# A graph network with attention on one core: argument in node order, a new step order, one subtraction on VectorE

## The chip, the cores and the metric

One core of a Trainium2 chip runs the whole kernel in one launch. The metric is the device time of that launch in microseconds (us). TensorE is called PE in the profile, VectorE DVE, ScalarE ACT, GpSimd POOL, and SyncE, whose queue issues the DMAs, SP; PEld is TensorE's weight load.

## The reference, cut to what matters

The input x is (16, 512, 256): 16 batches of 512 nodes with 256 features, and one 0/1 adjacency of 512 x 512 for all of them.

```
h   = relu(layernorm(x))
for 4 heads:  Wh = h @ W[head];  e[i,j] = leaky(f1[i] + f2[j]), masked by adj
              out[head] = softmax(e) @ Wh                       # f1 = Wh.a1, f2 = Wh.a2
h   = elu(concat of the heads)                                  # 512 x 1024
out = elu(the same attention once more, one head, W_out)        # the "back" head
y   = relu(out @ w1 + b1) @ w2 + b2 + out
x   = x + layernorm(y) * gamma + beta
h   = relu(layernorm(x))
x   = x + deg * (h @ Wi + b) + adj @ (h @ Wj)                   # graph convolution
```

Everything is fp32. The large products are made of three fast products each, hi x hi + lo x hi + hi x lo, where hi is the value rounded by ScalarE's copy (type fp32r) and lo is what is left, value - hi.

## The kernel before, in words

A batch passes through some forty steps on TensorE. Its attention is cut into ten units: four heads with two halves of 256 rows each, and the back head with two halves. UNITS (L233) numbers them: 0 to 3 are heads 0 and 1, 4 and 5 the back head of the batch before, 6 to 9 heads 2 and 3.

Each engine has a table of steps written out by hand at the top of the file: (name, info, late). The tables are walked once per wave, and a step works in wave t on batch t - late. So several batches are in flight, each engine runs its table strictly in order, and semaphores hold a step until its operands are there. The order in which work meets is set by these five tables alone.

A unit's way: `rowmax` on VectorE (L619) adds the broadcast f2 row (tile f2bc) to the mask, writes arg, and takes the row's maximum; `rowmath` (L629) makes two small vectors of it; `args` on ScalarE (L435) applies the leaky slope and the exponential; `rinv` and `scale` on VectorE (L645, L649) normalize; `turn_p` on TensorE (L774) transposes arg into PSUM in eight pieces; `probs` on ScalarE (L447) and on VectorE (L638) split it into prob_hi and prob_lo; `attend` on TensorE (L784) multiplies, 24 matmuls; `elu_neg` and `elu_exp` on ScalarE (L456, L467) and `elu_out` on VectorE (L656) form elu. For the four front heads `hx` on ScalarE (L471) rounds it to hx_hi, and `hx_lo` on GpSimd (L376) subtracts to get hx_lo. `mix2` on TensorE (L801) multiplies these by W_out, 24 matmuls for each 128 rows; it waits for hx_lo of the last head, for the first half before its steps 0 and 1, for the second before 2 and 3.

There are three arg buffers, two f2bc rows, two prob buffers and two elu buffers. `elu_neg` waits until the hx_lo of the unit two before has been made. PSUM is four pairs of banks: each TensorE step takes the pair that was taken longest ago, and waits until its last user has been read out (take and lend, L732 to L739).

The columns of arg are not in node order. x is loaded with node c * 128 + p in chunk c, partition p, and the f2 row is written to DRAM as (q c), so that its four chunks are interleaved. The mask is made in the same interleaved order, `rowmax` works on plain rows, and `turn_p` takes every fourth column of arg for each transposed piece. The norms' powers, `add_b2`, `gamma` and `x_beta` also run on GpSimd (L370 to L396). VectorE has two kinds of elementwise work that matter here: instructions with one operand in PSUM (`probs`, `elu_out`, `m1`) and instructions with both in SBUF (`rowmax`, `x2`).

The other steps: `m1` (L762) makes Wh and f1, f2 of a head for two chunks of rows, 12 matmuls; `f2send` and `f2bcast` on SP (L317, L331) write the f2 column to DRAM and read it back on all partitions; `ffn1`, `ffn2` (L825, L834), `turn_in`, `turn_out`, `turn_gc` (transposes), `conv_in` (L854) and `conv` (L865) are the rest; `store` and `load_back` on SP (L343, L338) write xb and fill it with the next batch's x.

## Time and profile before

| | |
|---|---|
| time, median of 3 | 1514.7 us (1514.22 to 1515.41) |
| the profiled execution's own time | 1505.55 us |
| its span | 1503.5 us |
| PE busy | 1339.4 us (89%), 9944 matmuls |
| PE weight loads | 1260.0 us (84%) |
| DVE busy | 1190.4 us (79%) |
| ACT busy | 1083.5 us (72%) |
| POOL busy | 349.2 us (23%) |
| chain that ended last | PE 51%, DVE 35%, issue 6%, ACT 5%, POOL 2% |

Busy time is the union of an engine's instructions. A matmul's duration in the profile is longer than the distance to the next, since they are pipelined: the distance (0.12 us for 256 columns) is what one costs. The span runs from the first to the last recorded work; the own time adds what lies around it.

### The profile page before, as it was taken

How to read it: one execution, taken by the hardware profiler on the slowest of the kernel's cores; microseconds unless marked ns; L12 is line 12 of the kernel's file. 1: busy time of each engine (PE TensorE's matmuls, PEld its weight loads, DVE VectorE, ACT ScalarE, POOL GpSimd, SP SyncE). 2: the span in 40 equal slices, each digit the busy share in tenths (PEclk: the TensorE clock that was granted, in tenths of full speed). 3: DMA queues.
4: the chain of work that ended last, by engine and by line, in shares of the span. 5: the costliest groups of instructions: out<-in, count | busy, mean ns of one | idle time of the engine just before them, and what ended most of it. 6: DMA issues, size and time to landing. Idle time of an engine off the chain costs nothing.

```text
span 1503.5 us, 27090 instructions
## 1 busy us (share of the span) xinstructions
PE 1339.4 (89%) x9944; PEld 1260.0 (84%) x9944; DVE 1190.4 (79%) x2833; ACT 1083.5 (72%) x2037; POOL 349.2 (23%) x234
## 2 busy tenths in 40 slices
...
DMA packets 53091, 54.07 MB, mean 36 GB/s; under 512 B 14048, under 2 KB 41696, under 8 KB 52832
## 3 DMA queue, kind: packets, MB, share of 16 engines
...
## 4 chain that ended last, share of the span: by engine, by line
PE 51%; DVE 35%; issue 6%; ACT 5%; POOL 2%; DMA 2%; POOLq 0%; ACTq 0%; DVEq 0%; SPq 0%
PE ps L747 33%; DVE arg L625 12%; PE ps L780 5%; DVE prob_lo L606 4%; DVE arg L653 4%; PE ps L830 4%; PE ps L871 4%; PE ps L840 3%; DVE elu L661 2%; DVE zneg L633 2%; DVE whx_lo L606 2%; DVE st L587 1%; POOL hx_lo L378 1%; DVE xb L699 1%; PE ps L849 1%
## 5 line engine op out<-in xcount | busy, mean ns | idle before, releaser
L378 POOL TENSOR_TENSOR hx_lo<-elu,hx_hi 128x512 fp32r<-128x512 f32 x128 | 171.2, 1338 | 622.7 <-ACT hx_hi L474 622.7
L747 PE MATMUL ps<-prob_hi,whx_hi 128*128 128x256 f32 x1024 | 298.5, 291 | 11.4 <-DVE wk L661 7.6
L747 PE MATMUL ps<-prob_lo,whx_hi 128*128 128x256 f32 x1024 | 289.7, 283 | 0.0
L747 PE MATMUL ps<-prob_hi,whx_lo 128*128 128x256 f32 x1024 | 289.2, 282 | 0.0
L625 DVE CUSTOM_DVE_ANT_0 arg<-f2bc,mask 128x512 f32<-128x512 f32 x320 | 278.7, 907 | 1.9 <-DMA f2bc<-f_rows 1.6
L444 ACT ACTIVATE arg<-arg,nmax 128x512 f32<-128x512 f32 x320 | 227.7, 718 | 0.6 <-DVE nmax L636 0.5
L440 ACT ACTIVATE arg<-arg,fcol 128x512 f32<-128x512 f32 x320 | 213.5, 721 | 12.1 <-DVE gmax L625 12.1
L780 PE MATMUL ps<-ident,arg 128*128 128x128 f32 x1280 | 186.9, 290 | 36.9 <-DVE arg L653 32.4
L747 PEld LDWEIGHTS ps<-prob_hi,whx_hi 128*128 128x128 f32 x1024 | 196.1, 192 | 17.2 <-issue 9.7
L780 PEld LDWEIGHTS ps<-ident,arg 128*128 128x128 f32 x1280 | 170.6, 209 | 45.0 <-DVE arg L653 34.8
L450 ACT ACTIVATE prob_hi<-ps 128x1024 fp32r<-128x1024 f32 x160 | 163.4, 1021 | 58.7 <-PE ps L747 33.1
L606 DVE TENSOR_TENSOR prob_lo<-ps,prob_hi 128x1024 fp32r<-128x1024 f32 x160 | 194.7, 1217 | 12.5 <-ACT prob_hi L450 9.8
L747 PEld LDWEIGHTS ps<-prob_hi,whx_lo 128*128 128x128 f32 x1024 | 195.6, 191 | 0.4
L747 PEld LDWEIGHTS ps<-prob_lo,whx_hi 128*128 128x128 f32 x1024 | 195.5, 191 | 0.0
L747 PE MATMUL ps<-wo_hi,hx_hi 128*128 128x258 f32 x512 | 146.0, 285 | 22.9 <-POOL hx_lo L378 22.9
L653 DVE TENSOR_SCALAR arg<-arg,rinv 128x512 f32<-128x512 f32 x320 | 153.5, 521 | 1.9
L747 PE MATMUL ps<-wh_hi,hT_hi 128*128 128x258 f32 x512 | 150.9, 295 | 2.4 <-DVE hT_lo L606 2.4
L747 PE MATMUL ps<-wh_lo,hT_hi 128*128 128x258 f32 x512 | 145.8, 285 | 0.0
L747 PE MATMUL ps<-wh_hi,hT_lo 128*128 128x258 f32 x512 | 145.4, 284 | 0.0
L747 PE MATMUL ps<-wo_lo,hx_hi 128*128 128x258 f32 x512 | 144.4, 282 | 0.0
L747 PE MATMUL ps<-wo_hi,hx_lo 128*128 128x258 f32 x512 | 143.8, 281 | 0.0
L433 ACT ACTIVATE whx_hi<-ps 128x512 fp32r<-128x512 f32 x128 | 75.8, 592 | 88.5 <-PE ps L747 88.5
...
## 6 DMA issues: line engine op xcount, KB each, us to landing
...
f_rows<-fcol SPq DMA_DIRECT2D x80, 2.0 KB, 3.4
...
```

Of the source, the lines that this page charges most:

```text
L378: pool.tensor_tensor(out=hx[1][:, 2 * c.h:2 * c.h + 2, c.u * HN:(c.u + 1) * HN], in0=elu[:, c.buf, :, :], in1=hx[0][:, 2 * c.h:2 * c.h + 2 ...
L433: act.activation(whx[:, 2 * p:2 * p + 2, h, 0:F], pairs[c.pair][:, :, 0:F], ACT.Copy).then_inc(m1_hi, 1)
L440: act.activation(a[:, n, :], a[:, n, :], ACT.Prelu, bias=f1[:, n:n + 1], alpha=SLOPE).then_inc(arg_lin, 1)
L444: i = act.activation(a[:, n, :], a[:, n, :], ACT.Exp, bias=nmax[:, c.abuf, n:n + 1], accum_out=rsum[:, c.abuf, n:n + 1])
L450: act.activation(prob[0][:, c.buf, :, :].rearrange("p j i -> p (j i)"), pairs[c.pair][:, :, :].rearrange("p a n -> p (a n)"), ACT.Copy).th ...
L606: return dve.tensor_tensor(out=dst, in0=src, in1=hi.bitcast(fp32), op=ALU.subtract)
L625: dve.tensor_tensor_reduce(out=arg[:, c.abuf, n, :], in0=f2bc[:, head % F2S, :], in1=mask[:, 2 * c.u + n, :], scale=1.0, scalar=-3.0e38, o ...
L653: i = dve.tensor_scalar(arg[:, c.abuf, n, :], arg[:, c.abuf, n, :], rinv[:, c.abuf, n:n + 1], None, ALU.mult)
L747: i = pe.matmul(out, a, b_, start=(k == 0), stop=(k == n - 1))
L780: i = pe.transpose(p[:, j, n, :], arg[:, c.abuf, n, :].rearrange("p (q c) -> p c q", c=NC)[:, j, :], ident[:, :])
L830: i = pe.matmul(pairs[c.pair][:, o, :], w1_sb[:, k, o * P:(o + 1) * P], outT[:, k, :], start=(k == 0), stop=(k == KC - 1))
L871: i = pe.matmul(pairs[c.pair][:, n // 2, (n % 2) * F:(n % 2 + 1) * F], adjT[:, j, n * P:(n + 1) * P], mj, start=(j == 0 and s == 0), stop= ...
```

## The change

Three edits. The argument is in node order now: `rowmax` reads f2bc through a view that takes every fourth element, and writes plain rows; the mask is built in node order by one instruction; `turn_p` transposes plain slices. `hx_lo` is computed by VectorE, as a step in its table, and no more by GpSimd. All five tables have a new order, with some steps one or two waves later (`turn_in` 1 where it was 0, `conv` 6 where it was 4). ScalarE's table, left out below, has the same steps as before in a new order.

```diff
--- before.py
+++ after.py
@@ -5,52 +5,51 @@
 
 
 SP_STEPS = [
-    ("f2send", -1, 3), ("load", 0, 0), ("f2send", 2, 2), ("f2bcast", -1, 3), ("f2send", 3, 2), ("f2bcast", 2, 2),
-    ("store", 0, 5), ("f2bcast", 3, 2), ("f2send", 0, 1), ("load_back", 0, 4), ("f2send", 1, 1), ("f2bcast", 0, 1),
+    ("f2send", -1, 3), ("f2bcast", -1, 3), ("f2send", 2, 2), ("f2send", 3, 2), ("f2bcast", 2, 2), ("f2send", 0, 1),
+    ("load", 0, 0), ("f2bcast", 3, 2), ("store", 0, 5), ("load_back", 0, 4), ("f2send", 1, 1), ("f2bcast", 0, 1),
     ("f2bcast", 1, 1),
 ]
 PE_STEPS = [
-    ("m1", (1, 1), 1), ("attend", 5, 3), ("turn_p", 7, 2), ("attend", 6, 2), ("turn_p", 8, 2), ("m1", (2, 0), 1),
-    ("attend", 7, 2), ("m1", (2, 1), 1), ("turn_p", 9, 2), ("attend", 8, 2), ("turn_out", 0, 3), ("m1", (3, 0), 1),
-    ("attend", 9, 2), ("mix2", 0, 2), ("mix2", 1, 2), ("mix2", 2, 2), ("mix2", 3, 2), ("m1", (3, 1), 1), ("turn_p", 0, 1),
-    ("turn_in", 0, 0), ("ffn1", 0, 3), ("turn_gc", 0, 4), ("turn_p", 1, 1), ("attend", 0, 1), ("conv_in", 0, 4),
-    ("conv_in", 1, 4), ("turn_p", 2, 1), ("m1", (0, 0), 0), ("attend", 1, 1), ("turn_p", 3, 1), ("ffn2", 0, 3),
-    ("attend", 2, 1), ("m1", (0, 1), 0), ("conv", 0, 4), ("turn_p", 4, 2), ("attend", 3, 1), ("turn_p", 5, 2),
-    ("m1", (1, 0), 0), ("turn_p", 6, 1), ("attend", 4, 2),
+    ("conv", 0, 6), ("turn_p", 5, 4), ("m1", (1, 1), 2), ("turn_p", 6, 3), ("attend", 4, 4), ("turn_p", 7, 3),
+    ("attend", 5, 4), ("attend", 6, 3), ("turn_p", 8, 3), ("attend", 7, 3), ("turn_p", 9, 3), ("turn_out", 0, 4),
+    ("attend", 8, 3), ("m1", (2, 0), 2), ("m1", (2, 1), 2), ("attend", 9, 3), ("ffn1", 0, 4), ("mix2", 0, 3),
+    ("turn_gc", 0, 5), ("turn_p", 0, 2), ("mix2", 1, 3), ("mix2", 2, 3), ("mix2", 3, 3), ("ffn2", 0, 4), ("m1", (3, 0), 2),
+    ("m1", (3, 1), 2), ("turn_p", 1, 2), ("turn_in", 0, 1), ("conv_in", 0, 5), ("attend", 0, 2), ("turn_p", 2, 2),
+    ("turn_p", 3, 2), ("attend", 1, 2), ("m1", (0, 0), 1), ("m1", (0, 1), 1), ("conv_in", 1, 5), ("attend", 2, 2),
+    ("turn_p", 4, 3), ("m1", (1, 0), 1), ("attend", 3, 2),
 ]
 ACT_STEPS = [
...
 DVE_STEPS = [
-    ("m1", (1, 1), 3), ("elu_out", 5, 5), ("probs", 7, 4), ("rinv", 9, 4), ("scale", 9, 4), ("elu_out", 6, 4),
-    ("probs", 8, 4), ("m1", (2, 0), 3), ("elu_out", 7, 4), ("m1", (2, 1), 3), ("rowmax", 0, 3), ("probs", 9, 4),
-    ("elu_out", 8, 4), ("rowmath", 0, 3), ("norm_gc", 0, 6), ("rowmax", 1, 3), ("rowmath", 1, 3), ("rowmax", 2, 3),
-    ("elu_out", 9, 4), ("rowmath", 2, 3), ("m1", (3, 0), 3), ("mix2", 0, 4), ("rinv", 0, 3), ("scale", 0, 3), ("rinv", 1, 3),
-    ("norm_gc_out", 0, 6), ("scale", 1, 3), ("mix2", 1, 4), ("m1", (3, 1), 3), ("probs", 0, 3), ("rowmax", 3, 3),
-    ("turn_in", 0, 2), ("rinv", 2, 3), ("rowmath", 3, 3), ("turn_gc", 0, 6), ("scale", 2, 3), ("probs", 1, 3),
-    ("norm_in", 0, 1), ("conv_in", 0, 6), ("rinv", 3, 3), ("elu_out", 0, 3), ("scale", 3, 3), ("conv_in", 1, 6),
-    ("probs", 2, 3), ("rowmax", 4, 4), ("rowmath", 4, 4), ("m1", (0, 0), 2), ("rowmax", 5, 4), ("rowmath", 5, 4),
-    ("probs", 3, 3), ("elu_out", 1, 3), ("rowmax", 6, 3), ("ffn2", 0, 5), ("rinv", 4, 4), ("rowmath", 6, 3),
-    ("norm_ff", 0, 5), ("scale", 4, 4), ("rinv", 5, 4), ("elu_out", 2, 3), ("m1", (0, 1), 2), ("conv", 0, 6),
-    ("norm_ff_out", 0, 5), ("scale", 5, 4), ("rowmax", 7, 3), ("rinv", 6, 3), ("norm_in_out", 0, 1), ("scale", 6, 3),
-    ("probs", 4, 4), ("rowmath", 7, 3), ("elu_out", 3, 3), ("probs", 5, 4), ("rowmax", 8, 3), ("m1", (1, 0), 2),
-    ("rinv", 7, 3), ("rowmath", 8, 3), ("scale", 7, 3), ("probs", 6, 3), ("x2", 0, 5), ("elu_out", 4, 4), ("rowmax", 9, 3),
-    ("rowmath", 9, 3), ("rinv", 8, 3), ("scale", 8, 3),
+    ("x2", 0, 6), ("elu_out", 4, 5), ("probs", 7, 4), ("rinv", 9, 4), ("scale", 9, 4), ("elu_out", 5, 5), ("elu_out", 6, 4),
+    ("probs", 8, 4), ("rowmax", 0, 3), ("hx_lo", 6, 4), ("elu_out", 7, 4), ("probs", 9, 4), ("rowmath", 0, 3),
+    ("rowmax", 1, 3), ("hx_lo", 7, 4), ("norm_gc", 0, 6), ("elu_out", 8, 4), ("rowmax", 2, 3), ("norm_gc_out", 0, 6),
+    ("rinv", 0, 3), ("hx_lo", 8, 4), ("rowmath", 1, 3), ("m1", (2, 0), 3), ("scale", 0, 3), ("m1", (2, 1), 3),
+    ("elu_out", 9, 4), ("rowmath", 2, 3), ("rowmax", 3, 3), ("hx_lo", 9, 4), ("rowmath", 3, 3), ("turn_gc", 0, 6),
+    ("norm_in", 0, 2), ("rinv", 1, 3), ("mix2", 0, 4), ("scale", 1, 3), ("rinv", 2, 3), ("rinv", 3, 3),
+    ("norm_in_out", 0, 2), ("scale", 2, 3), ("mix2", 1, 4), ("scale", 3, 3), ("probs", 0, 3), ("ffn2", 0, 5),
+    ("norm_ff", 0, 5), ("m1", (3, 0), 3), ("m1", (3, 1), 3), ("probs", 1, 3), ("turn_in", 0, 2), ("conv_in", 0, 6),
+    ("rowmax", 4, 4), ("rowmath", 4, 4), ("rowmax", 5, 4), ("elu_out", 0, 3), ("probs", 2, 3), ("rowmax", 6, 3),
+    ("probs", 3, 3), ("rowmath", 5, 4), ("rinv", 4, 4), ("elu_out", 1, 3), ("scale", 4, 4), ("hx_lo", 0, 3),
+    ("m1", (0, 0), 2), ("conv_in", 1, 6), ("m1", (0, 1), 2), ("rowmath", 6, 3), ("rowmax", 7, 3), ("rinv", 5, 4),
+    ("norm_ff_out", 0, 5), ("elu_out", 2, 3), ("hx_lo", 1, 3), ("rowmath", 7, 3), ("rinv", 6, 3), ("scale", 5, 4),
+    ("probs", 4, 4), ("scale", 6, 3), ("m1", (1, 0), 2), ("conv", 0, 6), ("elu_out", 3, 3), ("rowmax", 8, 3), ("rinv", 7, 3),
+    ("rowmath", 8, 3), ("probs", 5, 4), ("scale", 7, 3), ("m1", (1, 1), 2), ("hx_lo", 2, 3), ("rowmax", 9, 3),
+    ("probs", 6, 3), ("rowmath", 9, 3), ("rinv", 8, 3), ("hx_lo", 3, 3), ("scale", 8, 3),
 ]
 POOL_STEPS = [
-    ("hx_lo", 7, 4), ("hx_lo", 8, 4), ("norm_gc", 0, 6), ("add_b2", 0, 5), ("hx_lo", 9, 4), ("norm_in", 0, 1),
-    ("hx_lo", 0, 3), ("hx_lo", 1, 3), ("norm_ff", 0, 5), ("gamma", 0, 5), ("hx_lo", 2, 3), ("x_beta", 0, 5), ("hx_lo", 3, 3),
-    ("hx_lo", 6, 3),
+    ("norm_ff", 0, 6), ("gamma", 0, 6), ("x_beta", 0, 6), ("norm_gc", 0, 6), ("norm_in", 0, 2), ("add_b2", 0, 5),
 ]
 
 
@@ -373,11 +372,6 @@
                     pool.tensor_tensor(out=rstd[k][:, :], in0=mv[k][:, :, 1], in1=mhalf[:, :], op=ALU.pow).then_inc(ln_rstd[k], 1)
                 return step
 
-            def hx_lo_(c):
-                pool.wait_ge(hx_hi, head_unit(c.b, c.h, c.u) + 1)
-                pool.tensor_tensor(out=hx[1][:, 2 * c.h:2 * c.h + 2, c.u * HN:(c.u + 1) * HN], in0=elu[:, c.buf, :, :],
-                                   in1=hx[0][:, 2 * c.h:2 * c.h + 2, c.u * HN:(c.u + 1) * HN].bitcast(fp32), op=ALU.subtract).then_inc(hx_lo, 1)
-
             def add_b2(c):
                 if c.b == 0:
                     pool.wait_ge(ld[LD_B2], 16)
@@ -398,7 +392,7 @@
             for l in (LD_G, LD_BE):
                 pool.wait_ge(ld[l], 16)
             pool.wait_ge(s_setup, 1)
-            run_all(POOL_STEPS, {"norm_in": norm("in"), "hx_lo": hx_lo_, "add_b2": add_b2, "x_beta": x_beta_,
+            run_all(POOL_STEPS, {"norm_in": norm("in"), "add_b2": add_b2, "x_beta": x_beta_,
                                  "norm_ff": norm("ff"), "gamma": gamma_, "norm_gc": norm("gc")})
 
         @block.scalar
@@ -516,10 +510,7 @@
 
             dve.wait_ge(ld[LD_ADJ], 16)
             link(dve.tensor_copy(adj_f, adj_f.bitcast(i32)))
-            for n in range(NC):
-                i = dve.tensor_scalar(mask[:, n, :].rearrange("p (q c) -> p c q", c=NC), adj_f[:, n, :].rearrange("p (c q) -> p c q", c=NC),
-                                      0.0, 1.0, ALU.is_gt, ALU.mult)
-            i.then_inc(s_adj, 1)
+            dve.tensor_scalar(mask[:, :, :], adj_f, 0.0, 1.0, ALU.is_gt, ALU.mult).then_inc(s_adj, 1)
             dve.wait_ge(s_adj, 1)
             link(dve.tensor_reduce(out=cnt, in_=mask[:, :, :], axis=AX.X, op=ALU.add))
             link(dve.tensor_scalar(lone, cnt, 0.0, 2.0 * BIG, ALU.is_equal, ALU.mult))
@@ -622,7 +613,9 @@
                 dve.wait_ge(f2_spread[head % F2S], 16 * (head // F2S + 1))
                 wait(dve, p_turned, c.unit - ARGS + 1)
                 for n in range(2):
-                    dve.tensor_tensor_reduce(out=arg[:, c.abuf, n, :], in0=f2bc[:, head % F2S, :], in1=mask[:, 2 * c.u + n, :],
+                    dve.tensor_tensor_reduce(out=arg[:, c.abuf, n, :].rearrange("p (c q) -> p c q", c=NC),
+                                             in0=f2bc[:, head % F2S, :].rearrange("p (q c) -> p c q", c=NC),
+                                             in1=mask[:, 2 * c.u + n, :].rearrange("p (c q) -> p c q", c=NC),
                                              scale=1.0, scalar=-3.0e38, op0=ALU.add, op1=ALU.max,
                                              accum_out=gmax[:, c.abuf, n:n + 1]).then_inc(max_made, 1)
 
@@ -666,6 +659,11 @@
                 ps, n = pairs[c.pair], 2 * c.info
                 lo(w2l[:, n:n + 2, :], ps[:, :, 0:F], w2x[:, n:n + 2, 0:F]).then_inc(m2_lo, 1)
                 dve.tensor_copy(fcol2[:, :, n:n + 2].rearrange("p s n -> p n s"), ps[:, :, F:FA]).then_inc(m2_read, 1)
+
+            def hx_lo_(c):
+                dve.wait_ge(hx_hi, head_unit(c.b, c.h, c.u) + 1)
+                dve.tensor_tensor(out=hx[1][:, 2 * c.h:2 * c.h + 2, c.u * HN:(c.u + 1) * HN], in0=elu[:, c.buf, :, :],
+                                   in1=hx[0][:, 2 * c.h:2 * c.h + 2, c.u * HN:(c.u + 1) * HN].bitcast(fp32), op=ALU.subtract).then_inc(hx_lo, 1)
 
             def ffn2(c):
                 dve.wait_ge(f2_done, c.b + 1)
@@ -701,7 +699,7 @@
 
             run_all(DVE_STEPS, {"norm_in": norm("in", xin, x_loaded, 16), "norm_in_out": norm_out("in"), "turn_in": turn_in, "m1": m1,
                                 "rowmax": rowmax, "rowmath": rowmath, "rinv": rinv_, "scale": scale, "probs": probs,
-                                "elu_out": elu_out_, "mix2": mix2, "ffn2": ffn2,
+                                "elu_out": elu_out_, "hx_lo": hx_lo_, "mix2": mix2, "ffn2": ffn2,
                                 "norm_ff": norm("ff", wk, y_ready, 1), "norm_ff_out": norm_out("ff"), "x2": x2,
                                 "norm_gc": norm("gc", xb, x2_ready, 1), "norm_gc_out": norm_out("gc"),
                                 "turn_gc": turn_gc, "conv_in": conv_in_, "conv": conv})
@@ -777,7 +775,7 @@
                 p = pairs[c.pair][:, :, :].rearrange("p a n -> p (a n)").rearrange("p (j n i) -> p j n i", j=NC, n=2)
                 for j in range(NC):
                     for n in range(2):
-                        i = pe.transpose(p[:, j, n, :], arg[:, c.abuf, n, :].rearrange("p (q c) -> p c q", c=NC)[:, j, :], ident[:, :])
+                        i = pe.transpose(p[:, j, n, :], arg[:, c.abuf, n, j * P:(j + 1) * P], ident[:, :])
                 i.then_inc(p_turned, 1)
                 lend((c.pair,), (prob_lo, c.unit + 1))
 
```

## Rows read from the trace of the kernel before

**Rows 1.** Windows, steady stretch: PE, PEld, DVE, ACT, POOL busy us; clock; DMA; GB/s
```profile
150.00:1350.00 1200.00, 1133.98 (x8556) 1071.47 (x8555) 1002.24 (x2355) 933.81 (x1768) 296.52 (x190) 1.00 0.13 33
```

**Rows 2.** Timeline of GpSimd, one line twelve batches apart: start us, us
```profile
270.00 2.43 POOL L385 TENSOR_TENSOR wk<-wk,b_bc 128x1024 f32<-128x1024 f32 x1
...
1312.87 2.43 POOL L385 TENSOR_TENSOR wk<-wk,b_bc 128x1024 f32<-128x1024 f32 x1
```

**Rows 3.** Chain of waits, 700 to 800 us: start us, us, engine, what, count
```profile
702.26 0.60 DVE arg L625
...
716.79 0.98 PE ps L780 x8
717.77 0.87 PE ps L758 x8
718.64 3.44 PE ps L830 x8
...
728.65 1.40 PE ps L747 x6
...
732.84 0.95 PE ps L780 x8
733.79 4.32 PE ps L747 x36
...
739.07 3.46 PE ps L840 x16
...
746.84 3.85 PE ps L871 x32
```

**Rows 4.** Who waited for whom, whole run: us in total, times, longest us
```profile
POOL hx_lo L378 <- ACT hx_hi L474: 622.7, 113, 26.1
...
PE ps L747 <- POOL hx_lo L378: 22.9, 14, 2.0
...
PE ps L747 <- DVE elu L661: 18.2, 14, 1.4
```

**Rows 5.** Instructions of single lines: ns min/median/max, first and last start us, form
```profile
L780 PEld LDWEIGHTS ps<-ident,arg x1280: 195/209/231, 62.3 to 1427.9; 128*128 128x128 f32 x183
...
L758 PEld LDWEIGHTS ps<-ident,xin x128: 139/143/231, 37.6 to 1241.1; 128*128 128x128 f32 x128
...
L625 DVE CUSTOM_DVE_ANT_0 arg<-f2bc,mask x320: 674/685/2899, 55.7 to 1419.3; 128x512 f32<-128x512 f32 x160
...
L679 DVE TENSOR_TENSOR xb<-xb,wk x16: 1207/1208/2280, 246.3 to 1473.6; 128x1024 f32<-128x1024 f32 x16
...
L378 POOL TENSOR_TENSOR hx_lo<-elu,hx_hi x128: 1262/1292/1678, 85.2 to 1393.5; 128x512 fp32r<-128x512 f32 x128
```

**Rows 6.** Timeline of VectorE in the setup: start us, us
```profile
6.14 1.23 DVE L518 CAST arg<-arg 128x2048 f32<-128x2048 int32 x1 [6.14 <-DMA arg<-in_adj]
7.40 2.45 DVE L520 TENSOR_SCALAR mask<-arg 128x512 bf16<-128x512 f32 x4
```

**Rows 7.** Timelines of VectorE and GpSimd, two places where they meet
```profile
703.23 2.87 DVE L625 CUSTOM_DVE_ANT_0 arg<-f2bc,mask 128x512 f32<-128x512 f32 x1
...
703.11 2.44 POOL L385 TENSOR_TENSOR wk<-wk,b_bc 128x1024 f32<-128x1024 f32 x1
...
783.18 1.77 DVE L625 CUSTOM_DVE_ANT_0 arg<-f2bc,mask 128x512 f32<-128x512 f32 x1
...
782.73 1.67 POOL L378 TENSOR_TENSOR hx_lo<-elu,hx_hi 128x512 fp32r<-128x512 f32 x1 [1.11 <-ACT hx_hi L474]
```

**Rows 8.** Groups by line, VectorE: count, busy us, mean ns, idle before us
```profile
L625 DVE CUSTOM_DVE_ANT_0 arg<-f2bc,mask 128x512 f32<-128x512 f32 x320 | 278.7, 907 | 1.9 <-DMA f2bc<-f_rows 1.6
```

**Rows 9.** Chain of waits, the end of the run
```profile
1464.35 2.91 DMA out_x<-xb
...
1493.44 0.61 ACT h2T_hi L500
...
1494.81 4.11 PE ps L871 x32
```

More of the change, by code:

```diff
@@ L20 @@
+    ("turn_gc", 0, 5), ("turn_p", 0, 2), ("mix2", 1, 3), ("mix2", 2, 3), ("mix2", 3, 3), ("ffn2", 0, 4), ("m1", (3, 0), 2),
+    ("m1", (3, 1), 2), ("turn_p", 1, 2), ("turn_in", 0, 1), ("conv_in", 0, 5), ("attend", 0, 2), ("turn_p", 2, 2),
+    ("turn_p", 3, 2), ("attend", 1, 2), ("m1", (0, 0), 1), ("m1", (0, 1), 1), ("conv_in", 1, 5), ("attend", 2, 2),
+    ("turn_p", 4, 3), ("m1", (1, 0), 1), ("attend", 3, 2),
 ]
 ACT_STEPS = [
-    ("probs", 4, 3), ("norm_ff_out", 0, 4), ("elu_neg", 3, 2), ("hx", 2, 2), ("elu_exp", 3, 2), ("probs", 5, 3),
@@ L23 @@
-    ("m1", (1, 0), 1), ("args", 7, 2), ("probs", 6, 2), ("elu_neg", 4, 3), ("hx", 3, 2), ("elu_exp", 4, 3), ("args", 8, 2),
-    ("elu_neg", 5, 3), ("m1", (1, 1), 1), ("probs", 7, 2), ("elu_exp", 5, 3), ("args", 9, 2), ("elu_neg", 6, 2),
-    ("elu_exp", 6, 2), ("probs", 8, 2), ("m1", (2, 0), 1), ("elu_neg", 7, 2), ("hx", 6, 2), ("m1", (2, 1), 1),
-    ("elu_exp", 7, 2), ("hx", 7, 2), ("probs", 9, 2), ("elu_neg", 8, 2), ("elu_exp", 8, 2), ("turn_out", 0, 3), ("hx", 8, 2),
-    ("elu_neg", 9, 2), ("m1", (3, 0), 1), ("elu_exp", 9, 2), ("hx", 9, 2), ("norm_in_out", 0, 0), ("args", 0, 1),
@@ L28 @@
-    ("mix2", 0, 2), ("args", 1, 1), ("mix2", 1, 2), ("norm_gc_out", 0, 4), ("m1", (3, 1), 1), ("probs", 0, 1),
-    ("turn_in", 0, 0), ("args", 2, 1), ("turn_gc", 0, 4), ("ffn1", 0, 3), ("probs", 1, 1), ("args", 3, 1), ("elu_neg", 0, 1),
-    ("elu_exp", 0, 1), ("conv_in", 0, 4), ("conv_in", 1, 4), ("probs", 2, 1), ("hx", 0, 1), ("m1", (0, 0), 0),
-    ("elu_neg", 1, 1), ("probs", 3, 1), ("elu_exp", 1, 1), ("args", 4, 2), ("args", 5, 2), ("elu_neg", 2, 1), ("hx", 1, 1),
-    ("elu_exp", 2, 1), ("m1", (0, 1), 0), ("args", 6, 1),
+    ("args", 4, 4), ("probs", 3, 3), ("elu_neg", 1, 3), ("m1", (0, 0), 2), ("hx", 0, 3), ("elu_exp", 1, 3),
@@ new lines @@
+    ("conv_in", 1, 6), ("m1", (0, 1), 2), ("args", 5, 4), ("elu_neg", 2, 3), ("hx", 1, 3), ("elu_exp", 2, 3), ("args", 6, 3),
+    ("probs", 4, 4), ("elu_neg", 3, 3), ("m1", (1, 0), 2), ("elu_exp", 3, 3), ("args", 7, 3), ("probs", 5, 4), ("hx", 2, 3),
+    ("hx", 3, 3), ("m1", (1, 1), 2), ("norm_ff_out", 0, 5), ("probs", 6, 3), ("args", 8, 3), ("elu_neg", 4, 4),
+    ("probs", 7, 3), ("elu_exp", 4, 4), ("elu_neg", 5, 4), ("args", 9, 3), ("elu_neg", 6, 3), ("elu_exp", 5, 4),
+    ("elu_exp", 6, 3), ("probs", 8, 3), ("hx", 6, 3), ("elu_neg", 7, 3), ("elu_exp", 7, 3), ("probs", 9, 3),
```

5 lines of the change are left out of this document (added).

## The prediction

> **What bounds the kernel now.** I read the windows first, then the chain of waits inside one batch, then the table of who waited for whom, then the groups by line, and last the two engines that touch each other, instruction by instruction.
>
> Away from the ends TensorE is busy 94% of the time at full clock, VectorE 84%, ScalarE 78%, GpSimd 25% [rows 1]. The batches repeat: the same GpSimd instruction starts at 270.00 and, twelve batches on, at 1312.87 [rows 2], so one batch takes 1042.87 / 12 = 86.9 us.
>
> How much of this is TensorE work? From the chain: `attend` issues 24 matmuls, 36 take 4.32 us, so 2.88 us; ten of them 28.8. Eight `m1` are 96 such matmuls, 11.5; four `mix2` another 96, 11.5. Ten `turn_p` at 0.96 are 9.6. `ffn1` 3.44, `ffn2` 3.46, `conv` 3.85, `conv_in` 4 x (1.40 + 0.12 for its bias) = 6.1, three other turns at 0.87, 2.6 [rows 3]. Sum 80.9. So 86.9 - 80.9 = 6.0 us per batch is idle, and the engine is the bound, but not at its floor. VectorE is busy 1002.24 us in 1200, 72.6 us per batch [rows 1]: 14 us of room.
>
> What ends TensorE's idle time: over the run 22.9 us for `hx_lo` from GpSimd (14 times, about 1.6 us each), 18.2 us for `elu_out` (14 times) [rows 4].
>
> **The change part by part.**
>
> *Transposes of plain slices.* The weight loads of `turn_p` read every fourth element now: 209 ns median, against 143 ns for the loads of plain slices of `xin` [rows 5]. Loads overlap matmuls, so this difference isn't the price. The chain has it: eight transposes of arg take 0.95 to 0.98 us, eight of `xin` 0.87 [rows 3]. That is 0.09 us x 160 = 14 us of the bounding engine. Ends: 0 (the loads hide wholly, and the step in the chain is some other start-up) and 160 x 0.11 = 18. I take 14, the middle of the two rows.
>
> *rowmax reads f2bc at every fourth element.* 320 instructions, now 685 ns median, 0.60 us apart in the chain [rows 3, 5]. The trace has no VectorE instruction of size with an input strided so. Ends: 0, and twice the time, a bound from the difference between 0.60 and 1.20 us. I take 0, since the instruction isn't quick enough to press on its reads: it passes 2048 elements in 4 x 0.60 = 2.4 us, where the plain conversion of 2048 took 1.23. And the nearest strided VectorE row, the writing of mask with gaps, takes 2.45 us for four, 0.61 apart, like the unstrided rowmax [rows 6]. The high end is a rival below.
> The Trainium skill speaks against this choice: SBUF — State Buffer, section "Door 1: The DMA port swizzle", says that an SBUF line has 16 bytes and that at least two hits on a line are needed for full bandwidth, while it also calls a stride of four fp32 free. By the first sentence the edit costs VectorE time, by the second nothing. The trace shows only TensorE's loads slower (209 against 143), and that does not decide it.
>
> *mask in natural order.* Four instructions, 2.45 us, become one over the same 2048 elements [rows 6]. The plain conversion beside it took 1.23 us, so up to 1.2 are saved, at the start, where all waits for VectorE. I take 1; ends 0 and 1.2.
>
> *hx_lo leaves GpSimd.* 128 instructions of 1292 ns median go [rows 5]. On VectorE one costs 0.60 us: 512 elements with two fp32 inputs; x2, the same form with 1024, takes 1208 ns [rows 5]. 128 x 0.60 = 77 us added, 4.8 per batch. It also takes a load off VectorE: a two-input instruction from SBUF stands still while GpSimd works. Rowmax takes 2.87 us when it starts 0.12 after a 2.44 us addition on GpSimd, and 1.77 us beside an `hx_lo` [rows 7]. By line, rowmax loses (907 - 685) ns x 320 = 71 us to this [rows 5, 8]. `hx_lo` makes up 128 x 1.29 = 165 us of GpSimd's large instructions, the additions 48 x 2.44 = 117, so its part by time is 58%, 41 us. So net VectorE gets 77 - 41 = 36 us, 2.2 per batch: 72.6 becomes 74.8. The rest of the lock stays, with three GpSimd operations of this kind per batch (`add_b2`, `gamma`, `x_beta`), and `hx_lo` can now be hit by it itself; ends of the net load 77 - 71 = 6 and 77 + 117, every addition's time lost in full.
> The skill's SBUF — State Buffer, section "Who interferes with whom", gives the rule: a VectorE instruction with two SBUF inputs and a GpSimd one that reads SBUF exclude each other for the whole instruction. The trace agrees (2.87 us against a median of 685 ns), and by it the moved subtraction becomes one more victim of the additions that stay.
>
> *The wait for hx_lo.* The last batch half needed is unit 9, and `mix2` 2 needs it. Before, two `mix2` stand between `attend` 9 and `mix2` 2: 5.7 us, and the operand comes 1.6 us late. In the new order `ffn1`, two `mix2`, `turn_gc` and one `turn_p` stand there: 3.44 + 5.74 + 0.87 + 0.96 = 11.0 us. The path (two ScalarE passes, elu_out, hx, hx_lo) took 5.7 + 1.6 = 7.3 and gets 0.7 shorter, as 0.60 replaces 1.27. VectorE has only `rowmath` 2, `rowmax` 3 (1.5 us) ahead of `hx_lo` 9. So 22.9 us go, and 2 us of room are left. Ends 0 and 23.
>
> *The order otherwise.* Between `turn_p` and `attend` of a unit TensorE has other work that must cover ScalarE's 1.02 and VectorE's 1.22 us. Summed over the tables with the durations above: unit 0 before, `turn_in`, `ffn1`, `turn_gc`, `turn_p`, 6.1 us; after, three `mix2`, `ffn2`, two `m1`, `turn_p`, `turn_in`, `conv_in`, 19.8. Mean of the ten units 7.7 before, 9.5 after; the smallest 5.1 and 4.6. A PSUM pair is taken again after at least 3.3 us of other work in both. So the average handoff is looser, the tightest no better, while VectorE is fuller. I book -3 us, ends -55 (period 82.5, 2.5 idle) and +30.
>
> *SP.* `load_back` now follows `store` directly, and waits for its 2.9 us [rows 9] with `f2send` 1 and `f2bcast` 0 and 1 behind it. Before, `f2bcast` 3 and `f2send` 0 stood between. `rowmax` 0, which needs the broadcast, comes in the next wave, some 20 us later; nothing is booked, and if that cover failed it would be up to 3 us a batch.
>
> *The ends.* `turn_in` of a batch to its `conv` is 4.3 waves in both tables, so the fill stays. In the drain `ffn2` of the last batch moves ahead of the conv of the one before. Before, it covers the wait of `conv` for the last lo part; the very last batch shows this wait bare, from 1493.44 to 1494.81, 1.4 us [rows 9]. The chain from that conv over store, reload, the addition and the last conv is unchanged. Booked +1.
>
> Sum: -14 - 23 - 1 - 3 + 1 = -40 us, that is about 2.6 us less per batch. The profiled execution took 1505.55 us, 1503.5 of it span, and would take 1465.5. The median of the runs is 1514.7, 9 us above it; with the same difference 1474.7, say 1475.
>
> **The rivals.**
>
> A, *VectorE becomes the bound through the strided read*. For it: TensorE's strided load is 209 / 143 = 1.46 times as long [rows 5]. At 1.46, 0.28 us x 320 = 88 us, 5.5 per batch: VectorE 80.3, TensorE 80.0, and with the 6 us of idling that the leader has today 86.3: 1514.7 - 0.6 x 15 = 1506. At twice the time 192 us, 12.0 per batch, 86.8 + 6 = 92.8: 5.9 x 15 = +88, 1603. It decides from about 0.3 us per instruction. Against it: at 0.60 us the instruction takes longer than its reads need, by the conversion's row. The two-hits rule of the Trainium skill (SBUF — State Buffer, section "Door 1: The DMA port swizzle") would be its cause.
>
> B, *VectorE, in order, waits for ScalarE's hx*. GpSimd could sit out 622.7 us for `hx_hi` [rows 4]; VectorE can't. Place: between `elu_out` u and `hx_lo` u the new table has 1.5 us (units 8, 9) to 10 us of other work, and ScalarE must get through hx in its own queue. If each of 128 waits cost 0.7 us, that is 5.6 per batch, VectorE 80.4, and as TensorE's waits for it grow with each late release, the period 86.4 + 1.1 (half of the 2.2 added in work) = 87.5: 0.6 x 15 = +9, 1524. Below about 0.3 us each it disappears in the room.
>
> C, *the idle time only moves*: the 6 us come back elsewhere, only the transposes stay: 1514.7 - 14 = 1501, or with a worse drain 1513.
>
> D, *the looser order pays in full*: period 82.5, 1514.7 - 4.4 x 15 - 9 = 1440.
>
> **How the numbers follow.** Forecast 0.50 (1455 to 1500), A 0.20, B 0.12, C 0.06, D 0.12. A difference is told from none at 0.2%, 3 us. Faster: 0.50 + 0.12 + 0.03 of A (a small penalty) + 0.03 of C = 0.68; same 0.02 + 0.02 + 0.03 = 0.07; slower 0.15 + 0.10 = 0.25. Range 1435 to 1540: below, all of D but its tail; above, all of B and the lower part of A. The forecast's own range is 1455 to 1500.
>
> **What would show it.** Right: rowmax's median still near 685 ns; `turn_p` loads near 143 ns; no TensorE wait for hx_lo above a few us in total; VectorE near 75 us per batch; one batch about 84.3 us by the starts of the GpSimd addition. Wrong: a rowmax median of 0.9 us or more (A); a VectorE row "hx_lo waits for hx_hi" of over 80 us (B); the transposes' step unchanged, or a batch still at 86 us with no engine fuller (C).

## The result, and the profile after

The changed kernel takes 1554.93 us (median of 4, 1554.57 to 1555.77) beside 1514.46 us for the kernel before: ratio 1.0268, interval 1.0252 to 1.0284. It is slower; 1475 us was forecast, and the range ended at 1540. The profiled execution has a span of 1553.1 us.

The windows of the steady stretch in the changed kernel, as in [rows 1]: time of PE, PEld, DVE, ACT, POOL, then clock.

```profile
150.00:1350.00 1200.00, 1115.05 (x8383) 1047.92 (x8382) 1101.56 (x2414) 922.54 (x1728) 139.31 (x77) 0.99 0.12 33
```

VectorE is busy 92% of the time now, TensorE 93% with fewer matmuls in the same 1200 us (8383 for 8556). The batches, by the same GpSimd addition as in [rows 2], ten batches apart in the changed kernel:

```profile
297.19 2.70 POOL L379 TENSOR_TENSOR wk<-wk,b_bc 128x1024 f32<-128x1024 f32 x1
...
1189.64 2.70 POOL L379 TENSOR_TENSOR wk<-wk,b_bc 128x1024 f32<-128x1024 f32 x1
```

(1189.64 - 297.19) / 10 = 89.2 us per batch, for 86.9. VectorE's part of it is 1101.56 / 1200 x 89.2 = 81.9 us. The single lines, answering to [rows 5], ns min/median/max:

```profile
L616 DVE CUSTOM_DVE_ANT_0 arg<-f2bc,mask x320: 1051/1096/3195, 54.6 to 1460.5; 128x512 f32<-128x512 f32 x160
...
L778 PEld LDWEIGHTS ps<-ident,arg x1280: 137/141/231, 62.8 to 1470.8; 128*128 128x128 f32 x183
```

Rowmax went from 685 to 1096 ns; the loads of the transposes from 209 to 141. In the chain of waits between 700 and 800 us a rowmax instruction takes 1.01 to 1.03 us, for 0.60 in [rows 3]; eight transposes take 0.87 in the second of the two rows, for 0.95 to 0.98:

```profile
706.22 1.03 DVE arg L616
707.26 1.01 DVE arg L616
...
713.21 1.07 PE ps L778 x8
...
717.45 0.87 PE ps L778 x8
```

Who waited, answering to [rows 4]: no row of TensorE's matmuls waiting for hx_lo is left (its weight loads keep 4.2 us). Its largest wait is now that of `turn_p` for `scale`, the last VectorE step of a unit before it. The second row goes the other way: rowmax waits until a transpose has freed an arg buffer. So neither engine bounds the kernel alone; of the chain that ended last TensorE has 47% and VectorE 45%, for 51% and 35% before.

```profile
PE ps L778 <- DVE arg L646: 54.5, 21, 11.2
...
DVE arg L616 <- PE ps L778: 52.3, 30, 2.8
...
PE ps L745 <- DVE prob_lo L597: 41.4, 29, 2.7
```

And VectorE's setup, as in [rows 6]:

```profile
7.54 1.23 DVE L513 TENSOR_SCALAR mask<-arg 128x2048 bf16<-128x2048 f32 x1
```

The mask costs 1.23 us for 2.45, as booked (1 us). VectorE's `hx_lo` (L665) is 845 ns in the mean and waited only 1.7 us in all for hx_hi:

```profile
L665 DVE TENSOR_TENSOR hx_lo<-elu,hx_hi 128x512 fp32r<-128x512 f32 x128 | 108.2, 845 | 1.7 <-ACT hx_hi L468 1.7
```

### The profile page after: what moved, and what is told of

Read it like the earlier page. It is cut to its first block, busy times and chain, and to the rows that moved or that the text cites. A ratio compares the mean times of both kernels' runs of the same rounds, so it can differ in the third digit from the quotient of the medians.

```text
span 1553.1 us, 27087 instructions
## 1 busy us (share of the span) xinstructions
PE 1353.6 (87%) x9944; PEld 1265.6 (81%) x9944; DVE 1330.9 (86%) x2958; ACT 1092.4 (70%) x2037; POOL 172.8 (11%) x106
## 4 chain that ended last, share of the span: by engine, by line
PE 47%; DVE 45%; issue 4%; ACT 2%; DMA 2%; POOL 0%; DVEq 0%; POOLq 0%; SPq 0%; ACTq 0%
PE ps L745 32%; DVE arg L616 13%; DVE prob_lo L597 6%; DVE arg L646 5%; PE ps L778 4%; PE ps L869 4%; PE ps L828 4%; DVE hx_lo L665 3%; DVE st L578 2%; DVE shift_in L592 2%; DVE elu L654 1%; DVE whx_lo L597 1%; DVE h2T_lo L597 1%; PE ps L847 1%; DVE w2x_lo L597 1%
## 5 line engine op out<-in xcount | busy, mean ns | idle before, releaser
L616 DVE CUSTOM_DVE_ANT_0 arg<-f2bc,mask 128x512 f32<-128x512 f32 x320 | 346.7, 1123 | 56.8 <-PE ps L778 52.3
L745 PE MATMUL ps<-prob_hi,whx_hi 128*128 128x256 f32 x1024 | 298.9, 292 | 37.2 <-DVE prob_lo L597 27.2
L745 PE MATMUL ps<-prob_hi,whx_lo 128*128 128x256 f32 x1024 | 293.3, 286 | 0.0
L778 PE MATMUL ps<-ident,arg 128*128 128x128 f32 x1280 | 170.4, 280 | 60.8 <-DVE arg L646 54.5
L778 PEld LDWEIGHTS ps<-ident,arg 128*128 128x128 f32 x1280 | 146.4, 144 | 67.9 <-DVE arg L646 59.3
L745 PEld LDWEIGHTS ps<-prob_hi,whx_lo 128*128 128x128 f32 x1024 | 199.7, 195 | 1.2
L745 PEld LDWEIGHTS ps<-prob_lo,whx_hi 128*128 128x128 f32 x1024 | 199.6, 195 | 0.0
L459 ACT ACTIVATE elu<-ps 128x512 f32<-128x512 f32 x160 | 94.9, 593 | 103.7 <-PE ps L745 71.7
L646 DVE TENSOR_SCALAR arg<-arg,rinv 128x512 f32<-128x512 f32 x320 | 166.8, 563 | 0.7
L745 PEld LDWEIGHTS ps<-wo_hi,hx_hi 128*128 128x128 f32 x512 | 96.6, 189 | 19.2 <-issue 15.0
```

The costliest lines, as they stand in the source:

```text
L459: act.activation(elu[:, c.buf, :, :], pairs[c.pair][:, :, 0:F], ACT.Relu, scale=-1.0).then_inc(elu_neg, 1)
L616: dve.tensor_tensor_reduce(out=arg[:, c.abuf, n, :].rearrange("p (c q) -> p c q", c=NC), in0=f2bc[:, head % F2S, :].rearrange("p (q c) -> ...
L646: i = dve.tensor_scalar(arg[:, c.abuf, n, :], arg[:, c.abuf, n, :], rinv[:, c.abuf, n:n + 1], None, ALU.mult)
L745: i = pe.matmul(out, a, b_, start=(k == 0), stop=(k == n - 1))
L778: i = pe.transpose(p[:, j, n, :], arg[:, c.abuf, n, j * P:(j + 1) * P], ident[:, :])
```

## The experiments

Theory 1: the read of f2bc at 16-byte steps lengthens rowmax, and VectorE's added time is the loss. Theory 2: hx_lo in VectorE's queue, or the new order, costs the time. The runs below were made on several chips. The kernel before, run beside each, took 1510.7 to 1514.9 us in the median, so differences between two runs are uncertain by up to some 4 us; each ratio is against the kernel before on the same chip.

**The argument edit, alone and left out.** `b_arg_only` is the kernel before with the strided rowmax, the mask in one instruction, and plain transposes. `c_no_arg` is the changed kernel with these three undone:

```diff
-                    dve.tensor_tensor_reduce(out=arg[...].rearrange("p (c q) -> p c q", c=NC), in0=f2bc[...].rearrange("p (q c) -> p c q", c=NC), ...
+                    dve.tensor_tensor_reduce(out=arg[:, c.abuf, n, :], in0=f2bc[:, head % F2S, :], in1=mask[:, 2 * c.u + n, :],
-   pe.transpose(p[:, j, n, :], arg[:, c.abuf, n, j * P:(j + 1) * P], ident[:, :])
+   pe.transpose(p[:, j, n, :], arg[:, c.abuf, n, :].rearrange("p (q c) -> p c q", c=NC)[:, j, :], ident[:, :])
```

> The kernel before with the argument edit alone: strided rowmax, mask in one instruction, plain transposes; hx_lo on GpSimd and the old order. Theory 1: VectorE goes from 72.6 to about 72.6 + 8.2 = 80.8 us per batch, next to TensorE's 80.0, in an order made for 72.6: slower than before by 1 to 4%, 1530 to 1575 us. Theory 2: the edit alone costs next to nothing, 1500 to 1520 us.

> The changed kernel without the argument edit: plain rowmax on interleaved rows, old mask, strided transposes; hx_lo on VectorE and the new order stay. Theory 1: 1475 + 14 for the transposes = about 1489 us. Theory 2: above 1530 us. Against the run with the row in node order it gives the price of the strided weight loads alone, 14 us by my sum, 0 to 18 at the ends.

Alone it takes 1640.98 us (ratio 1.0855, 1.0813 to 1.0896), worse than expected by either theory: 128 us slower than before for 320 x 0.41 = 131 us of longer rowmax. Not all of this is VectorE's time. The profiled execution has a mean granted clock of 0.941 over 1632.6 us, for 0.982 over 1503.5 before. As an estimate from these four numbers, the lower clock can have cost at most (1 - 0.941) x 1632.6 = 96 us for 27 before, 69 of the 128; how much it did cost wasn't measured. Left out: 1501.99 us (0.9925, 0.9901 to 0.9949). So the argument edit is the loss, and the rest of the change a gain. Repeated, on another chip:

> The best version so far that computes the reference, again and with more rounds: new order, hx_lo on VectorE, the argument edit left out. 0.7 to 0.8% faster than before if the first measurement holds, about 1502 us; within 0.3% if it was its chip.

1499.31 us (0.9896, 0.9881 to 0.9910). It is the fastest of these kernels that computes the reference.

**Plain rows, everything else as changed.** `i_plain_read` changes the rowmax call alone, from the first line of the diff above to the second. The f2 row still comes interleaved, so its attention adds f2 values of the wrong nodes, and only its time counts.

> The changed kernel with rowmax reading plain rows of f2bc, while the f2 row is still sent interleaved: the attention adds f2 values of the wrong nodes, all sizes and counts stay. Theory 1 (the step of 16 bytes on VectorE is the whole loss): rowmax 687 ns, and the time is that of the run without the argument edit less the strided weight loads, 1502 - 14 = 1488 us, 67 below the changed kernel. Its rival (plain slices in the transposes cost something of their own, or the clock): 1502 us or above. It also tells whether the 1699 us of the row in node order came from the sends of 4 bytes alone (then this run is near 1488) or from something else in it (then this run is above 1550).

1486.43 us (0.9827, 0.9806 to 0.9848). The only difference to the changed kernel is how rowmax reads, and it is worth 1554.93 - 1486.43 = 68.5 us. Theory 2 falls. The clock isn't behind it: the mean is 0.953 in this profile and 0.962 in that of the changed kernel. In this kernel (windows as above, and ten batches):

```profile
150.00:1350.00 1200.00, 1151.69 (x8786) 1096.30 (x8784) 1039.76 (x2536) 962.38 (x1816) 148.88 (x82) 0.98 0.12 35
```
```profile
287.08 2.71 POOL L379 TENSOR_TENSOR wk<-wk,b_bc 128x1024 f32<-128x1024 f32 x1
...
1134.80 2.73 POOL L379 TENSOR_TENSOR wk<-wk,b_bc 128x1024 f32<-128x1024 f32 x1
```

84.8 us per batch, VectorE 1039.76 / 1200 x 84.8 = 73.5. And TensorE's two waits:

```profile
PE ps L743 <- DVE prob_lo L597: 41.5, 17, 3.5
...
PE ps L776 <- DVE arg L644: 18.9, 9, 9.1
```

The wait for prob_lo is the same as in the changed kernel (41.4); the one for `scale` is 18.9 us for 54.5, and the 12 more times are about one per batch. VectorE has 17% of the chain that ended last, for 45%.

**What a step costs, by itself.** Two kernels of single operations.

> VectorE instructions alone, 512 elements each, twelve of a kind, all else left out (the output is a copy of x). The fused add and max with an fp32 input at a step of 1, 2, 3, 4 and 8 elements, with the output at a step of 2 and 4, with the bf16 input at a step of 4 and 8, and as the changed kernel has it (step 4 in four passes of 128); a subtraction with steps 1 and 4; a scaling with steps 1, 2 and 4. Theory 1, in the form that a read at 16 bytes pays on each element: steps 1 to 3 at 685 ns, 4 and 8 at about 1100. Its rival, that the split in four passes costs the time: step 4 at 685 and only the four passes at 1100. A third: any step over 1 pays.

> Single operations alone, all else left out (the output is a copy of x): VectorE subtraction with one input at a step of 1, 2, 3 and 4 fp32 elements and scaling at 1, 2 and 4, ScalarE copy at 1, 2, 3 and 4, GpSimd copy at 1, 2 and 4, and TensorE transposes in runs of eight with weights at a step of 1, 2 and 4. If the 16-byte step is a matter of the reads and not of the fused instruction, the subtraction goes from 0.60 to about 0.97 us apart as the fused one does, and the scaling (0.40 us) loses at least as much; ScalarE, at 0.72 us for 512, loses little or nothing; the transposes' weight loads go from about 141 to 209 ns between steps 1 and 4.

Lines of the second (VectorE subtraction and scaling, ScalarE and GpSimd copy; the last word is the step in fp32 elements; busy us, mean ns):

```profile
L69 ACT ACTIVATE copy_four<-big 128x512 f32<-128x512 f32 x12 | 13.0, 1156 | 0.1
L57 DVE TENSOR_TENSOR subtract_four<-big,other 128x512 f32<-128x512 f32 x12 | 12.6, 1105 | 0.1
L82 POOL COPY pool_four<-big 128x512 f32<-128x512 f32 x12 | 12.4, 1076 | 0.2
...
L57 DVE TENSOR_TENSOR subtract_three<-big,other 128x512 f32<-128x512 f32 x12 | 9.9, 894 | 0.1
L57 DVE TENSOR_TENSOR subtract_two<-big,other 128x512 f32<-128x512 f32 x12 | 7.5, 687 | 0.1
L57 DVE TENSOR_TENSOR subtract_one<-big,other 128x512 f32<-128x512 f32 x12 | 7.5, 686 | 0.1
L69 ACT ACTIVATE copy_two<-big 128x512 f32<-128x512 f32 x12 | 7.3, 686 | 0.1
L82 POOL COPY pool_two<-big 128x512 f32<-128x512 f32 x12 | 7.1, 634 | 0.2
L82 POOL COPY pool_one<-big 128x512 f32<-128x512 f32 x12 | 6.8, 615 | 57.9 <-DVE other L61 57.8
L69 ACT ACTIVATE copy_one<-big 128x512 f32<-128x512 f32 x12 | 6.6, 618 | 3.8 <-DVE other L52 3.7
L60 DVE TENSOR_SCALAR scale_four<-big 128x512 f32<-128x512 f32 x12 | 6.5, 611 | 0.1
L60 DVE TENSOR_SCALAR scale_two<-big 128x512 f32<-128x512 f32 x12 | 4.3, 423 | 0.1
L60 DVE TENSOR_SCALAR scale_one<-big 128x512 f32<-128x512 f32 x12 | 4.3, 421 | 0.1
```

A step of 8 bytes is free on VectorE (686 and 687 ns), one of 12 costs (894), one of 16 costs 1.6 times (1105). All three engines pay for 16 bytes; ScalarE and GpSimd also pay a little for 8 (618 to 686 and 615 to 634 ns). The fused instruction of rowmax in the first kernel does the same, at steps of 1, 3 and 4 elements, and then with a bf16 input at 8 and at 16 bytes:

```profile
11.48 0.69 DVE L54 CUSTOM_DVE_ANT_0 fused_read<-big,small 128x512 f32<-128x512 f32 x1
...
27.80 0.83 DVE L54 CUSTOM_DVE_ANT_0 fused_read<-big,small 128x512 f32<-128x512 f32 x1
...
39.73 1.06 DVE L54 CUSTOM_DVE_ANT_0 fused_read<-big,small 128x512 f32<-128x512 f32 x1
...
86.24 0.69 DVE L54 CUSTOM_DVE_ANT_0 fused_halfread<-big,bigh 128x512 f32<-128x512 f32 x1
...
86.97 1.06 DVE L54 CUSTOM_DVE_ANT_0 fused_halfread<-big,bigh 128x512 f32<-128x512 f32 x1
```

A step of 8 elements takes 1.07 us, like 4; an output at steps of 2 and 4 fp32 elements 0.69 and 1.06. Bytes count, not elements, and for this instruction it doesn't matter which operand it is or whether the pattern has four passes (1.06 us as well).

TensorE differs. The second kernel also has 64 transposes each with weights at a step of 1, 2 and 4 fp32 elements. Their loads (ns min/median/max, first and last start us; the windows cut off one or two):

```profile
L92 PEld LDWEIGHTS ps<-ident,big x63: 139/140/153, 30.0 to 36.8; 128*128 128x128 f32 x63
L92 PEld LDWEIGHTS ps<-ident,big x63: 196/209/209, 37.0 to 44.4; 128*128 128x128 f32 x63
L92 PEld LDWEIGHTS ps<-ident,big x62: 209/209/212, 44.7 to 52.0; 128*128 128x128 f32 x62
```

Its loads cost as much at 8 bytes as at 16 (209 ns, for 140 plain), and the transposes stand 0.12 us apart at both, for 0.11. So the 209 ns of [rows 5] were no measure of a 16-byte step on another engine.

**Is it VectorE's time alone?** Added behind each rowmax of `i_plain_read`, with nothing strided:

```diff
+                    wait(dve, s_junk, 2 * c.unit + n - 1)
+                    dve.memset(junk[:, n, :], 0.0).then_inc(s_junk, 1)          # o_dummy
+                    dve.tensor_reduce(out=junk[:, n:n + 1], in_=mask[:, n, 0:288], axis=AX.X, op=ALU.max).then_inc(s_junk, 1)   # p_reduce, in its place
```

> The run with plain rows in rowmax (1486 us), plus a fill of 416 bf16 elements into a scratch tile behind each of the 320 rowmax instructions: about 0.35 to 0.40 us of VectorE time that reads nothing and that nobody waits for by itself, in place of the 0.36 us (0.976 - 0.614) that the strided read adds to each. Theory 1 (the loss is VectorE's time and nothing else): 1550 to 1560 us, like the changed kernel. Its rival (the strided read also disturbs others, as SBUF traffic, or by holding the lock against GpSimd longer): well below, 1500 to 1535 us.

1495.59 us (0.9879, 0.9856 to 0.9901). That looked like the rival, but the fill was three times too small: VectorE's busy time rose by 41.6 us (1204.0 to 1245.6), not by some 115. Hence two more. `p_reduce` has a larger filler; `q_half` has none, and the strided read in the first of each unit's two rowmax instructions only:

> The run with plain rows in rowmax (1486 us), plus a reduction over 288 elements of the mask behind each of the 320 rowmax instructions, about 0.36 us of VectorE each, for which nothing waits. Its busy time should rise by some 115 to 130 us, as in the changed kernel. Theory 1 (the loss is VectorE's time): 1540 to 1560 us. Its rival (the strided read does something beyond its time): below 1525 us.

> The changed kernel with the strided read in the first of each unit's two rowmax instructions only, the second on plain rows (its values are of the wrong nodes): half of the added 131 us. If the loss grows in proportion, 1486 + 34 = 1520 us. If VectorE has room for the first part and the loss starts behind it, 1495 to 1510, as the small fill (42 us of busy time for 9 us of run) hints.

1539.67 us (1.0187, 1.0164 to 1.0209) and 1513.64 us (1.0016, 1.0003 to 1.0030). The page's totals of VectorE in `i_plain_read`, `q_half`, `p_reduce` and the changed kernel are 1204.0, 1265.1, 1314.9 and 1330.9 us.

| added to VectorE, us | run longer by, us |
|---|---|
| 41.6 (fill) | 9.2 |
| 61.1 (half the strided reads) | 27.2 |
| 110.9 (reduction, nothing strided) | 53.2 |
| 126.9 (changed kernel) | 68.5 |

The first 40 us cost a fifth of themselves. What comes above them costs 0.63 in the reduction, 0.70 in the changed kernel and 0.92 in the half. These runs were on different chips; by their ratios to the kernel before (1.0268, 1.0187, 1.0016 and 0.9879, each less 0.9827, times 1514.5) the changed kernel is 67 us longer, the reduction 55, the half 29 and the fill 8. The line through the fill and the reduction then gives 65 us at 126.9 and 21 at 61.1. So time on VectorE that has nothing to do with strides explains the changed kernel's loss to 2 us. That the half lies 8 us above the line isn't settled; its runs spread from 1509.5 to 1518.1.

**The other parts.** `j_old_plain_turn` is the kernel before with the plain slices in turn_p alone (its columns and nodes no longer match, so only its time counts). `k_new_pool` is `c_no_arg` with hx_lo on GpSimd, in a GpSimd table that keeps the order of its other steps. `l_old_dve` is the kernel before with hx_lo as VectorE steps, shown by the step that each stands behind:

```diff
+ DVE: ("m1",(2,0),3), ("hx_lo",6,4) ... ("rowmax",0,3), ("hx_lo",7,4) ... ("norm_gc",0,6), ("hx_lo",8,4) ... ("m1",(3,0),3), ("hx_lo",9,4)
+      ("conv_in",1,6), ("hx_lo",0,3) ... ("ffn2",0,5), ("hx_lo",1,3) ... ("probs",4,4), ("hx_lo",2,3) ... ("scale",7,3), ("hx_lo",3,3)
```

> The kernel before with plain slices in the transposes and nothing else changed: the columns of the attention are permuted against the nodes, all sizes and counts stay. Booked in the prediction: 14 us less than before (0.09 us x 160), ends 0 and 18. If the order absorbs it in other waits, 0 to 5 us.

> The new order without the argument edit and with hx_lo on GpSimd again, in a GpSimd table in which each hx_lo stands where VectorE's table had it. VectorE sheds 77 us and gets back some 40 of the lock. If the move of hx_lo was what made the 11 us that the run without the argument edit gained, this one is at 1513 us or above; if the order made them, at 1495 to 1502.

> The kernel before with hx_lo as a VectorE step in the old order, each one step or a few behind its elu_out. Against before it changes that alone. TensorE's 22.9 us of waits for hx_lo go or shrink; VectorE gets 36 us net. If the move pays by itself, 1490 to 1505 us; if VectorE's queue then stands waiting for hx_hi in an order not made for it, 1520 to 1545, with hx_lo waits of over 50 us among VectorE's.

Plain slices: 1506.61 us (0.9955, 0.9940 to 0.9971), 7.7 less. New order with hx_lo on GpSimd: 1504.20 us (0.9942, 0.9919 to 0.9964), so the order alone makes 10 us. It also ends TensorE's wait for hx_lo by itself: `k_new_pool` has no such row, for 22.9 us before. The move of hx_lo gives 2 to 5 us on top (against `c_no_arg`, whose interval overlaps, and `c2_no_arg`, whose doesn't), and nothing per batch: 85.6 us with it on GpSimd, 85.8 and 85.9 on VectorE. The move in the old order: 1538.04 us (1.0173, 1.0148 to 1.0199), slower. There VectorE waits for hx_hi, and TensorE still for hx_lo:

```profile
DVE hx_lo L665 <- ACT hx_hi L467: 47.6, 64, 2.0
...
PE ps L745 <- DVE hx_lo L665: 15.1, 14, 1.1
```

**Two ways round the strided read.** `a_node_row` is the changed kernel with plain rows in rowmax, and sends the row to DRAM in node order:

```diff
-                sp.dma_start(f2_rows[head % 4].rearrange("(q c) -> q c", c=NC), column, ...
+                sp.dma_start(f2_rows[head % 4].rearrange("(c q) -> q c", c=NC), column, ...
```

> The changed kernel, with the f2 row sent to DRAM in node order, so that rowmax reads plain rows and arg is still in node order. Theory 1 (the strided read made VectorE the bound): rowmax falls from 1096 back to about 685 ns, VectorE loses 320 x 0.41 = 131 us of work, and the kernel comes to about 1475 us, faster than before by 2.6% or so. Theory 2 (hx_lo in VectorE's queue, or the new order, is what costs): rowmax is short again but the time stays above 1530 us. The f2 sends have 512 pieces of 4 bytes where they had 128 of 16; if that counts, f2_rows<-fcol lands later than in 1.9 us.

1698.80 us (1.1224, 1.1189 to 1.1258), the slowest of all, though rowmax is at 687 ns. It differs from `i_plain_read` by this line alone, and costs 212 us. From its waits and its chain between 700 and 800 us:

```profile
DVE arg L616 <- DMA f2bc<-f_rows: 190.6, 48, 16.1
```
```profile
736.35 10.93 DMA f_rows<-fcol
747.34 4.31 DMA f2bc<-f_rows
```

The send of 2 KB in 512 pieces takes 8 to 11 us here, where 128 pieces of 16 bytes took 2.5 from issue to landing (median of `i_plain_read`; 1.9 in the changed kernel, 3.4 before), and VectorE stands 190.6 us for the broadcast, for 4.7 in `i_plain_read`. This run's clock is lower too (0.91 for 0.95).

`m_act_turn` lets ScalarE put the row in order once per head, with one f2bc buffer and two of the turned row (and, to make room, the selector of the conv's bias as one column, read with a step of zero):

```diff
+                act.activation(f2n[:, head % F2S, :].rearrange("p (c q) -> p c q", c=NC), f2bc[:, :].rearrange("p (q c) -> p c q", c=NC), ACT.Copy).then_inc(f2_turned, 1)
```

> The changed kernel with the row put in node order once per head (80 times) by a ScalarE copy that reads every fourth element, instead of in each of the 320 rowmax instructions; f2bc is one buffer and the turned row has two, and the bias selector of the conv is read with a step of zero to make room. Theory 1: rowmax back at 687 ns, plain transposes kept, ScalarE gets 80 x 0.7 to 1.1 us = 56 to 88 us, 3.5 to 5.5 per batch on an engine with 16 us of room: 1486 to 1500 us, at or below the 1502 of the run without the argument edit and below before. If ScalarE's queue then holds its args or elu steps back behind the broadcast, up to 1520.

1600.54 us (1.0594, 1.0563 to 1.0625). The copy is 1132 ns, and ScalarE's queue stands 84.5 us before it for the broadcast, which now waits for the single buffer. My price of 0.7 to 1.1 us was about right, but the run is 114 us longer than `i_plain_read`. VectorE waits 94.8 us for ScalarE's elu, for 15.0 there, and the clock is 0.94 for 0.95. I put the loss down to these waits; how much is the buffer, the place in the queue, the selector or the clock wasn't told apart.

## Why the prediction was wrong

The step that failed is "rowmax reads f2bc at every fourth element": "I take 0". It cost 411 ns in the median (from start to start 0.98 us for 0.61 in `d_strides`), and 68.5 us of run. Without it, the same kernel runs in 1486.4, inside the forecast's own range (1455 to 1500) and 11 above its point. That is in part luck, as the terms below show: one other term was far too large and one far too small.

Why 0 was taken: I argued that the instruction is too slow to press on its reads. The scaling shows that this isn't how it adds up. It runs at 0.42 us and at 0.61 with the step; were the step only a floor under an instruction's time, rowmax at 0.61 apart would have stayed as it was. It got longer by 0.36 to 0.41 us, so the step adds to what is there; why by twice what the scaling pays isn't known. And the strided row that I took as the nearest, the mask with gaps, is bf16 at 4 elements: 8 bytes, which is free for every operand of the fused instruction that was tried. No row of the kernel before had a 16-byte step on VectorE. The only 16-byte row was TensorE's weight load, 1.46 times as long; on VectorE it is 1.6, and on TensorE 8 bytes cost the same as 16, so that this row lay near was luck. The Trainium skill (SBUF — State Buffer, section "Door 1: The DMA port swizzle") has both sentences that I weighed: two hits on a 16-byte line for full speed, and a stride of 4 fp32 as free. VectorE's runs bear out the first: 8 bytes free, 16 not. They contradict the second.

Rival A had the mechanism, at 0.20. Its price: at 0.36 us of the 0.60 its own sum gives 7.2 us more per batch, 82.0 + 6 = 88.0 us; measured 81.9 for VectorE and 89.2 for the batch. So VectorE's load was right and the idling a bit larger. By its sum that is 1514.7 + 1.1 x 15 = 1531 us; measured 1554.9, of which 1.2 x 15 = 18 is the idling, and the rest lies at the ends.

The others, by their steps:

- Plain transposes, 14 booked: the loads fell to 141 ns and the chain to 0.87 us as read. Alone in the old order 7.7 us; in the new one, with the mask, 13 by `c2_no_arg` (1499.3 - 1486.4) and 16 by `c_no_arg`.
- hx_lo and the order: TensorE's wait for hx_lo vanished, as derived, but by the order: it is gone in `k_new_pool` with hx_lo still on GpSimd, and 15.1 us of it stay in `l_old_dve` with hx_lo on VectorE. So the 23 us booked for the wait and the 3 for the order belong together: 26 booked, 10 measured by the order and 2 to 5 by the move. The one was far too large, the other too small.
- VectorE's load from the move: 36 us net booked. VectorE's busy time over the run goes from 1206.2 (`k_new_pool`) to 1209.8 us (`c2_no_arg`) in the new order, and from 1190.4 to 1214.9 in the old one: 4 and 25 us. Per batch it came out at 73.5 us without the strided read, 74.8 booked. The stretching, summed over all VectorE instructions more than 0.25 us above their form's median, is 128 us before and 61 in the changed kernel, where 27 us of it are in `scale`, 21 in `hx_lo` and 8 in rowmax (71 before). The three large GpSimd instructions per batch that stay meet other victims now.
- Rival B (VectorE waiting for ScalarE's hx): not in the new order (1.7 us in all), but it happens in the old one (47.6 us, and 1538 us of run). The mechanism exists; the new table avoids it.
- The fill: booked as unchanged. At 150 us the changed kernel has begun 591 matmuls for 692 before; with plain rows 620, and 616 without the argument edit. So the new order starts later by itself, by some 72 matmuls or 10 us at the steady rate of 0.14 us each. The 2.1 us that it gains per batch (86.9 to 84.8) would make 32 us in 15 batches; the spans of the same two profiles differ by 17 (1503.5 to 1486.1).
- The clock: read as full, and so it was in the steady stretch. The prediction has no term for it, and it changed (last section).
